# Local attention on Trainium2: the matmuls that spread the inverse sums become transposes and move ahead of the value products

## The chip, the cores and the metric

The kernel runs on one core of one Trainium2 chip. The metric is the device time of one execution in microseconds (us). Before the change it is 3235.11 us, the median of 3 runs (3233.68 to 3237.66). TensorE is PE here (its weight loads are PEld), VectorE is DVE, ScalarE is ACT, GpSimd is POOL, and SP issues most DMAs.

## What is computed

The whole program is two gated blocks of cross attention and feed-forward over 2048 tokens of 256 numbers. Only the last part is touched: a local transformer of two layers, each with windowed attention and a feed-forward. Cut to what matters, the reference is:

```python
def local_attention(q, k, v):                 # q, k, v: 8 heads, 2048 tokens, 64 numbers
    bq = q.reshape(b, h, w, WINDOW, d) * QK_SCALE      # WINDOW = 128, so 16 windows
    bk, bv = look_around(bk), look_around(bv)          # the window before and this one
    sim = jnp.einsum('bhwid,bhwjd->bhwij', bq, bk)
    sim = jnp.where(mask, -jnp.finfo(sim.dtype).max, sim)
    attn = jax.nn.softmax(sim, axis=-1)
    out = jnp.einsum('bhwij,bhwjd->bhwid', attn, bv)

# in a layer:
q, k = l2norm(q) * qs, l2norm(k) * ksc
q, k = rotary_xpos(q, k)
o = local_attention(q, k, v)
x = x + o.transpose(0, 2, 1, 3).reshape(b, n, INNER) @ wo
```

## The kernel before, in words

`windowed_attention` (L1885) runs once for each of the two layers and goes over 16 windows of 128 tokens. Each engine has its own instruction list, written out by hand as a loop over `w`; semaphores (`after`, L1911) tie the lists together, and nothing but the order of calls in each list sets the order of work on that engine. The loop is a software pipeline: in turn `w` TensorE computes the scores of window `w`, projects q, k and v of window `w + 3`, mixes the output of window `w - 1` with `wo`, turns the rotated q and k of window `w + 1`, turns the input of window `w + 4`, and then ends window `w`: `turn_probs` (L1994), `apply` (L2006), `spread` (L2021). All of it but the projections is float32; the projections are split into float16 halves. From `w = 12` on there is no input to turn, from `w = 13` on nothing is projected, and from `w = 14` on DVE has no q and k to prepare.

The softmax is not divided before the values are applied. `exp` (ACT, `expo`, L2065) leaves the sum of each row and head in `sums`; DVE takes their reciprocals (`invert`, L2187); POOL copies each of them 64 times along the free axis (`expand`, L2325); and `spread` on TensorE brings this `expanded` tile into the layout of the output, which has the heads' numbers on the partitions and the tokens along the free axis. It writes PSUM bank 7, `OUT_BANK`, which the turned input also uses. ACT copies the bank to SBUF (`move_spread`, L2075), and DVE multiplies `apply`'s result in PSUM by it (`normalize`, L2193). `mix` needs that product, and DVE's masks of the next window's scores (`mask`, L2201) stand behind it in DVE's list.

`spread` waits for POOL (`expanded`) and for ACT's copies of the turned input (`in_moved`). `apply` waits for ACT's copy of V (`valued`) and for the two halves of the turned probabilities (`probs_moved`). `score` of the next window comes after `spread` in TensorE's list and waits for `moved` and `probs_moved`; after half of its products it signals `scored`, for which the first mask waits.

```python
# ACT, turn w:  move_spread(w - 1); expo(w, 0); expo(w, 1); move(w + 1); move_input(w + 4);
#               square(w + 3); move_probs(w, 0); value(w + 3); move_probs(w, 1); root(w + 3)
# DVE, turn w:  make_unit(w + 2); normalize(w - 1); mask, maxima (w, 0); mask, maxima (w, 1);
#               add(w - 1); straighten(w + 2); rotate(w + 2); invert(w); sum_squares(w + 3)
```

Of the kernel before, what the change touches and what calls it, by code (L numbers as in the profile page):

```python
# [22 lines left out]
P = 128  # L23
# [1814 lines left out]
SCORE_BANK, QK_BANK, V_BANK, OUT_BANK = 3, 0, 2, 7  # L1838
# [46 lines left out]
def windowed_attention(nc, m, name, Z, pw, wm, w, l, s):  # L1885

    base = l * ST
    with ExitStack() as own:
# [16 lines left out]
        expanded = sb("expanded", [P, 4, 2, LD])  # L1905
# [5 lines left out]
        def after(engine, sem, count):  # L1911
            if count > 0:
                engine.wait_ge(s[sem], count)

        with nc.Block() as block:
# [5 lines left out]
            def _(pe):  # L1921
                def score(w):

                    after(pe, "moved", base + w + 1)
                    after(pe, "probs_moved", 2 * (base + w))
                    if w == 0:
                        after(pe, "united", base + 2)
                    last_slot, slot = (w - 1) % K_RING, w % K_RING
                    for c in range(4):
                        for e in range(2):  # L1930
                            rows = slice(64 * e, 64 * e + 64)
                            bank, at = SCORE_BANK + c // 2 * 2 + e, c % 2 * 2 * P
                            if last_slot < slot:
                                last = nc.tensor.matmul(m.PS[:, bank, at:at + 2 * P], qT[rows, c, :],
                                                        kT[rows, c, last_slot:slot + 1, :].rearrange("p o n -> p (o n)"),
                                                        start=True, stop=True)
                            else:
                                for j, sl in enumerate((last_slot, slot)):
                                    last = nc.tensor.matmul(m.PS[:, bank, at + j * P:at + (j + 1) * P], qT[rows, c, :],
                                                            kT[rows, c, sl, :], start=True, stop=True)  # L1940
                        if c % 2:
                            last.then_inc(s["scored"], 1)
# [10 lines left out]
                def project_qk(w):  # L1953

                    after(pe, "in_split", base + w + 1)

                    after(pe, "united", base + (w - 1 if w in (1, 2) else w))
                    for c in range(2):
                        last = project(m.PS[:, qk_bank(w) + c, :], w, c)
                    last.then_inc(s["qk_projected"], 1)  # L1960

                def project_v(w):

                    after(pe, "valued", base + w)
                    after(pe, "added", base + w - 3)
                    last = project(m.PS[:, V_BANK, :], w, 2)
                    last.then_inc(s["v_projected"], 1)

                def turn(w):

                    after(pe, "rotated", base + w + 1)
                    after(pe, "masked", 2 * (base + w) - 1)
                    for c in range(8):
                        last = nc.tensor.transpose(m.PS[:, SCORE_BANK + c // 4, (c % 4) * P:(c % 4 + 1) * P],
                                                   rotated[w % 2][:, c * P:(c + 1) * P], m.ident[:])
                    last.then_inc(s["turned"], 1)

                def turn_input(w):

                    after(pe, "normed", base + w - 4)  # L1980
                    after(pe, "in_moved", base + w)
                    for k in range(DK):
                        last = nc.tensor.transpose(m.PS[:, OUT_BANK, k * P:(k + 1) * P], Z[:, w, k * P:(k + 1) * P], m.ident[:])
                    last.then_inc(s["in_turned"], 1)

                def mix(w):

                    after(pe, "normed", base + w + 1)
                    for c in range(4):
                        last = nc.tensor.matmul(m.PS[:, V_BANK, 0:D], heads_outT[:, c, :], wo[:, c, :],  # L1990
                                                start=(c == 0), stop=(c == 3))
                    last.then_inc(s["mixed"], 1)

                def turn_probs(w, g):  # L1994

                    after(pe, "exped", 2 * (base + w) + g + 1)
                    if g == 0:
                        after(pe, "moved", base + min(w + 2, ST))
                    for p in range(4):
                        for kt in range(2):  # L2000
                            at = (p % 2 * 2 + kt) * P
                            last = nc.tensor.transpose(m.PS[:, SCORE_BANK + 2 * g + p // 2, at:at + P],  # L2002
                                                       probs[:, 4 * g + p, kt * P:(kt + 1) * P], m.ident[:])
                    last.then_inc(s["probs_turned"], 1)

                def apply(w):  # L2006


                    after(pe, "valued", base + min(w + 4, ST))
                    after(pe, "added", base + w)  # L2010
                    for c in range(4):
                        if c % 2 == 0:
                            after(pe, "probs_moved", 2 * (base + w) + c // 2 + 1)
                        for kt in range(2):
                            for e in range(2):
                                last = nc.tensor.matmul(m.PS[64 * e:64 * e + 64, V_BANK, c * P:(c + 1) * P],
                                                        V[:, (w - 1 + kt) % V_RING, 2 * c + e, :],
                                                        probsT[c // 2][:, c % 2 + 2 * e, kt, :], start=(kt == 0), stop=(kt == 1))
                    last.then_inc(s["applied"], 1)

                def spread(w):  # L2021

                    after(pe, "expanded", base + w + 1)
                    after(pe, "in_moved", base + min(w + 5, ST))
                    for c in range(4):
                        last = nc.tensor.matmul(m.PS[:, OUT_BANK, c * P:(c + 1) * P],
                                                expanded[:, c].rearrange("p e d -> p (e d)"), m.ident[:], start=True, stop=True)
                    last.then_inc(s["spread"], 1)

                turn_input(0)  # L2030
# [11 lines left out]
                for w in range(ST + 1):  # L2042
                    if inside(w):
                        score(w)
                    if inside(w + 3):
                        project_qk(w + 3)
                    if inside(w - 1):
                        if w == 1:
                            pe.wait_ge(s["rest_in"], 32 * (l + 1))
                        mix(w - 1)  # L2050
                    if inside(w + 1):
                        turn(w + 1)
                    if inside(w + 3):
                        project_v(w + 3)
                    if inside(w + 4):
                        turn_input(w + 4)
                    if inside(w):
                        for g in range(2):
                            turn_probs(w, g)
                        apply(w)  # L2060
                        spread(w)

            @block.scalar
            def _(act):
# [712 lines left out]
```

## Time and profile before

| | us |
|---|---|
| median of 3 runs | 3235.11 |
| the profiled execution's own time | 3229.91 |
| its span, from the first to the last instruction | 3227.8 |
| PE busy in the span | 2967.1 (92%) |
| DVE busy | 2208.0 (68%) |
| ACT busy | 1982.0 (61%) |
| POOL busy | 218.4 (7%) |
| mean granted TensorE clock | 0.975 of full speed |

The granted clock is a share of 2.4 GHz; a stretch at 1.2 GHz counts half. The first attention, which the change does not touch, takes some two thirds of the span. Windowed attention of the first layer lies at about 2435 to 2702 us, that of the second at about 2835 to 3098 us. A float32 matmul shows in the trace as two records for each one in the program, a transpose as one. A number in square brackets at the end of a row is the idle time of the engine just before it, with what ended it.

### The profile page before, as it was taken

How to read it: one execution, taken by the hardware profiler on the slowest of the kernel's cores; microseconds unless marked ns; L12 is line 12 of the kernel's file. 1: busy time of each engine (PE TensorE's matmuls, PEld its weight loads, DVE VectorE, ACT ScalarE, POOL GpSimd, SP SyncE). 2: the span in 40 equal slices, each digit the busy share in tenths (PEclk: the TensorE clock that was granted, in tenths of full speed). 3: DMA queues.
4: the chain of work that ended last, by engine and by line, in shares of the span. 5: the costliest groups of instructions: out<-in, count | busy, mean ns of one | idle time of the engine just before them, and what ended most of it. 6: DMA issues, size and time to landing. Idle time of an engine off the chain costs nothing. (4 is left out here: it accounts for less than half of the span.)

```text
span 3227.8 us, 71016 instructions
## 1 busy us (share of the span) xinstructions
PE 2967.1 (92%) x29442; PEld 1483.9 (46%) x29442; DVE 2208.0 (68%) x2752; ACT 1982.0 (61%) x2682; POOL 218.4 (7%) x325
## 2 busy tenths in 40 slices
PE   6999999999999999999999887999977887988878
PEld 3444444444444444444444563222235665556655
DVE  6888788878888888878788854000027775677756
ACT  5665655655656656556556424999965773267732
POOL 0000000000000000000000102000004223042200
PEclk8999999999999999999999898999998998999989
DMA  2000000000000000000000003110010001000000
GB/s 78 7 2 2 8 2 8 2 2 8 2 2 8 2 2 8 2 3 2 2 3 2 31 3 126 27 36 27 28 44 20 17 1 58 3 16 17 1 1 27
DMA packets 30033, 51.65 MB, mean 16 GB/s; under 512 B 6071, under 2 KB 22538, under 8 KB 28554
## 3 DMA queue, kind: packets, MB, share of 16 engines
q1 hardware_dynamic: 29706, 46.91, 4.6%
q8 instruction: 252, 4.13, 0.5%
q14 instruction: 75, 0.61, 0.1%
HBM read 41.04 MB, written 5.83 MB: 15 GB/s over the span
## 5 line engine op out<-in xcount | busy, mean ns | idle before, releaser
L734 ACT ACTIVATE a_probs<-PS 128x1024 f32<-128x1024 f32 x928 | 949.1, 1024 | 601.2 <-PE PS L489 597.4
L502 PE MATMUL PS<-a_probs,a_V 64*64 64x512 f32 x7424 | 977.8, 590 | 5.0 <-DVE a_heads_outT L915 3.6
L956 DVE TENSOR_TENSOR a_prob_sums<-a_prob_sums,a_probs 128x1024 f32<-128x1024 f32 x512 | 627.1, 1225 | 153.8 <-ACT a_probs L734 137.8
L953 DVE SCALAR_TENSOR_TENSOR a_prob_sums<-a_probs,a_valid,a_prob_sums 128x1024 f32<-128x1024 f32 x384 | 480.4, 1251 | 70.2 <-ACT a_probs L734 60.3
L489 PE MATMUL PS<-a_Q_hi,a_K_hi 64*64 64x512 f16 x3712 | 383.9, 381 | 5.0 <-ACT a_probs L734 4.7
L1772 ACT ACTIVATE c_probs<-PS 128x1024 f32<-128x1024 f32 (+1 forms) x416 | 382.8, 1080 | 8.3 <-PE PS L1691 6.7
L489 PE MATMUL PS<-a_Q_lo,a_K_hi 64*64 64x512 f16 x3712 | 383.5, 377 | 2.5 <-issue 2.5
L489 PE MATMUL PS<-a_Q_hi,a_K_lo 64*64 64x512 f16 x3712 | 381.1, 377 | 1.3 <-issue 1.3
L502 PEld LDWEIGHTS PS<-a_probs,a_V 64*64 64x64 f32 x7424 | 288.5, 133 | 164.1 <-issue 20.4
L489 PEld LDWEIGHTS PS<-a_Q_hi,a_K_hi 64*64 64x64 f16 x3712 | 118.4, 106 | 275.8 <-issue 270.7
L489 PEld LDWEIGHTS PS<-a_Q_hi,a_K_lo 64*64 64x64 f16 x3712 | 119.0, 107 | 228.3 <-issue 226.4
L1711 PE MATMUL PS<-c_probs,c_Vh 128*32 128x512 f32 (+1 forms) x1664 | 222.5, 607 | 0.3 <-ACT c_probs L1772 0.3
L1790 DVE COPY c_outT<-PS 128x512 f32<-128x512 f32 x16 | 11.1, 691 | 303.3 <-PE PS L1711 303.3
L1691 PE MATMUL PS<-c_Qop,c_Kop 64*128 64x512 f16 (+1 forms) x832 | 155.6, 390 | 34.6 <-ACT c_probs L1772 11.3
L2071 ACT ACTIVATE d_probs<-d_scores,d_minus_max 128x256 f32<-128x256 f32 x256 | 127.0, 497 | 88.2 <-DVE d_minus_max L2214 88.2
L489 PEld LDWEIGHTS PS<-a_Q_lo,a_K_hi 64*64 64x64 f16 x3712 | 120.0, 107 | 92.7 <-issue 7.8
L1691 PEld LDWEIGHTS PS<-c_Qop,c_Kop 64*128 64x128 f16 (+1 forms) x832 | 38.7, 94 | 250.9 <-ACT c_probs L1772 236.8
L923 DVE RECIPROCAL a_inverse<-PS 128x128 f32<-128x128 f32 x128 | 121.5, 950 | 27.1 <-PE PS L512 27.1
L71 POOL TENSOR_TENSOR b_W_lo<-b_W1T,b_W_hi 128x256 f16<-128x256 f32 x8 | 8.1, 1044 | 1830.9 <-DVE b_W_hi L67 1830.9
L2002 PE MATMUL PS<-ident,d_probs 128*128 128x128 f32 x512 | 70.3, 296 | 48.2 <-ACT d_kT L2086 41.5
L2310 POOL TENSOR_TENSOR d_crossed<-d_unit,d_tables 128x256 f32<-128x256 f32 x128 | 92.7, 758 | 147.8 <-DVE d_unit L2182 147.8
L2002 PEld LDWEIGHTS PS<-ident,d_probs 128*128 128x128 f32 x512 | 62.2, 153 | 56.2 <-issue 48.3
(325 smaller groups left out, 4227.5 us busy)
## 6 DMA issues: line engine op xcount, KB each, us to landing
c_Qop<-q_part SPq DMA_DIRECT2D x96, 64.0 KB, 2.3
c_Kop<-k_part SPq DMA_DIRECT2D x96, 50.0 KB, 2.0
d_raw<-in_l1f_w_dram SPq DMA_DIRECT2D x18, 256.0 KB, 3.2
d_tables<-in_rotary_dram SPq DMA_DIRECT2D x2, 2048.0 KB, 11.0
X<-in_x_dram SPq DMA_DIRECT2D x2, 1024.0 KB, 9.5
out_dram<-X SPq DMA_DIRECT2D x4, 512.0 KB, 3.5
c_cT<-in_ctxT_dram SPq DMA_DIRECT2D x1, 1601.0 KB, 6.4
a_probs<-in_ctx_dram SPq DMA_DIRECT2D x3, 512.0 KB, 5.0
```

The source lines that it names most:

```text
L489: last = nc.tensor.matmul(m.PS[64 * g:64 * g + 64, 2 * (n % 2) + h, :], k[rows, half_keys], q[rows, queries], start=(j == 0), stop=(j == l ...
L502: last = nc.tensor.matmul(m.PS[64 * h:64 * h + 64, PVB + g, :], V[e][rows, s, 64 * h:64 * h + 64], probs[n % 4][rows, h * BANK:(h + 1) * B ...
L734: nc.scalar.activation(probs[n % 4][:], m.PS[:, b0:b0 + 2, :].rearrange("p b c -> p (b c)"), ACT.Exp).then_inc(exped, 1)
L923: nc.vector.reciprocal(inverse[:, part], m.PS[:, TOTAL, part]).then_inc(inverted, 1)
L953: nc.vector.scalar_tensor_tensor(out=sums, in0=new, scalar=valid[:, s:s + 1], in1=sums, op0=ALU.mult, op1=ALU.add).then_inc(summed, 1)
L956: nc.vector.tensor_tensor(sums, sums, new, ALU.add).then_inc(summed, 1)
L1691: last = nc.tensor.matmul(m.PS[0:r, STEP_BANKS[n] + b, :], Kop[e][rows, c0:c0 + r], Qop[e][rows, q0:q0 + BANK], start=True, stop=True)
L1711: last = nc.tensor.matmul(m.PS[32 * q:32 * q + 32, 4 + e, :], Vh[e][0:r, t % CT, :], probs[2 * (t % 2) + q // 2][0:r, (q % 2) * BANK:(q % ...
L1772: nc.scalar.activation(probs[2 * (t % 2) + hp][0:r, :], m.PS[0:r, STEP_BANKS[n]:STEP_BANKS[n] + 2, :].rearrange("p b c -> p (b c)"), ACT.E ...
L2002: last = nc.tensor.transpose(m.PS[:, SCORE_BANK + 2 * g + p // 2, at:at + P], probs[:, 4 * g + p, kt * P:(kt + 1) * P], m.ident[:])
L2071: last = nc.scalar.activation(probs[:, p, :], scores[:, p, :], ACT.Exp, bias=minus_max[:, p:p + 1], accum_out=sums[:, p:p + 1])
L2310: last = nc.gpsimd.tensor_tensor(crossed[:, qk, :, a, :], unit[w % 2][:, qk, :, 1 - a, :], tables[:, 1, w, qk, a * 32:a * 32 + 32].unsquee ...
```

## The change

`spread` issues four transposes in place of four float32 matmuls with the same operands: `expanded` is the stationary operand and the identity the moving one, as before. And in TensorE's list `spread(w)` stands ahead of `apply(w)`, right behind `turn_probs(w, 1)`. No wait is added or removed; the lists of the other engines are as they were.

```diff
@@ -2023,8 +2023,8 @@
                     after(pe, "expanded", base + w + 1)
                     after(pe, "in_moved", base + min(w + 5, ST))
                     for c in range(4):
-                        last = nc.tensor.matmul(m.PS[:, OUT_BANK, c * P:(c + 1) * P],
-                                                expanded[:, c].rearrange("p e d -> p (e d)"), m.ident[:], start=True, stop=True)
+                        last = nc.tensor.transpose(m.PS[:, OUT_BANK, c * P:(c + 1) * P],
+                                                   expanded[:, c].rearrange("p e d -> p (e d)"), m.ident[:])
                     last.then_inc(s["spread"], 1)
@@ -2057,8 +2057,8 @@
                     if inside(w):
                         for g in range(2):
                             turn_probs(w, g)
+                        spread(w)
                         apply(w)
-                        spread(w)
```

TensorE's list at the end of an early window, with the turned input ahead and the next window's scores and projection behind (`d_probs` are the probabilities, `d_expanded` the copied inverse sums, `d_probsT` with `d_V` the value products, `d_kT` with `d_qT` the scores; x4 and the like count the program's operations):

```order
 L1983 MATMUL PS<-ident,d_Z 128x128 x2
 L2002 MATMUL PS<-ident,d_probs 128x128 x16
+L2026 MATMUL PS<-ident,d_expanded 128x128 x4
 L2016 MATMUL PS<-d_probsT,d_V 64x128 x16
-L2026 MATMUL PS<-ident,d_expanded 128x128 x4
 L1934 MATMUL PS<-d_kT,d_qT 128x256 x8
 L77 MATMUL PS<-qkv_hi,d_zw_lo 128x512
```

The four operations go from behind the value products to before them, so that the next window's scores follow the value products directly.

TensorE's list where a layer's projections have ended, from the close of window 12 to the close of window 13 (`d_wo` is the output matrix, `d_rotated` the rotated q and k):

```order
 L2002 MATMUL PS<-ident,d_probs 128x128 x16
+L2026 MATMUL PS<-ident,d_expanded 128x128 x4
 L2016 MATMUL PS<-d_probsT,d_V 64x128 x16
-L2026 MATMUL PS<-ident,d_expanded 128x128 x4
 L1934 MATMUL PS<-d_kT,d_qT 128x256 x8
 L1990 MATMUL PS<-d_wo,d_heads_outT 128x256 x4
 L1974 MATMUL PS<-ident,d_rotated 128x128 x8
 L2002 MATMUL PS<-ident,d_probs 128x128 x16
+L2026 MATMUL PS<-ident,d_expanded 128x128 x4
 L2016 MATMUL PS<-d_probsT,d_V 64x128 x16
-L2026 MATMUL PS<-ident,d_expanded 128x128 x4
```

The move is the same here, but no projections stand between the scores and the mix.

## Rows read from the trace of the kernel before

**Rows 1.** Windows: us, busy us per engine (PE, PEld, DVE, ACT, POOL), clock, DMA.
```profile
2542.29:2557.69 15.40, 13.78 (x110) 10.25 (x110) 12.13 (x17) 12.16 (x28) 4.54 (x8) 1.00 0.06 18
2650.06:2667.00 16.94, 12.04 (x90) 10.49 (x91) 9.17 (x11) 9.04 (x23) 3.52 (x6) 0.80 0.00 1
```

**Rows 2.** Timeline of ACT in one early window: start, duration, what [idle before].
```profile
2548.71 0.51 ACT L2071 ACTIVATE d_probs<-d_scores,d_minus_max 128x256 f32<-128x256 f32 x1 [0.31 <-DVE d_minus_max L2214]
...
2551.96 1.03 ACT L2104 ACTIVATE d_squares<-PS 128x1024 f32<-128x1024 f32 x1
...
2553.91 0.59 ACT L2111 ACTIVATE d_V<-PS 128x512 f32<-128x512 f32 x1
2554.39 1.03 ACT L2117 ACTIVATE d_probsT<-PS 128x1024 f32<-128x1024 f32 x1
...
2556.73 0.21 ACT L2124 ACTIVATE d_norms<-d_norms 128x16 f32<-128x16 f32 x1
2557.69 0.60 ACT L2079 ACTIVATE d_spread_in<-PS 128x512 f32<-128x512 f32 x1 [0.75 <-PE PS L2026]
```

**Rows 3.** Timeline of DVE, the window before and the start of the next.
```profile
2542.08 1.23 DVE L2182 TENSOR_TENSOR d_unit<-PS,d_norms 128x1024 f32<-128x1024 f32 x1
2543.22 0.68 DVE L2198 TENSOR_TENSOR d_heads_outT<-PS,d_spread_in 128x512 f32<-128x512 f32 x1
...
2556.98 0.17 DVE L2177 TENSOR_SCALAR d_norms<-d_norms 128x16 f32<-128x16 f32 x1 [1.68 <-ACT d_norms L2124]
```

**Rows 4.** Timeline of PE, and POOL's copy, in the same window as rows 2.
```profile
2551.70 0.74 POOL L2331 COPY d_expanded<-d_inverse 128x256 f32<-128x256 f32 x2 [5.54 <-DVE d_inverse L2191]
2551.89 1.94 PE L2002 MATMUL PS<-ident,d_probs 128*128 128x128 f32 x16 [0.90 <-ACT d_kT L2086]
2554.56 2.01 PE L2016 MATMUL PS<-d_probsT,d_V 128*64 128x128 f32 x32 [0.73 <-ACT d_V L2111]
2556.50 1.16 PE L2026 MATMUL PS<-ident,d_expanded 128*128 128x128 f32 x8
2557.59 2.00 PE L1934 MATMUL PS<-d_kT,d_qT 64*128 64x256 f32 x16
```

**Rows 5.** Who waited for L2026; what L2198 waited for (us, times).
```profile
  ACT d_spread_in L2079: 34.8, 32
...
  ACT d_spread_in L2079: 45.3, 6
```

**Rows 6.** Timeline, end of window 13 of the first layer.
```profile
2663.23 2.64 PE L2016 MATMUL PS<-d_probsT,d_V 128*64 128x128 f32 x32
2665.80 1.16 PE L2026 MATMUL PS<-ident,d_expanded 128*128 128x128 f32 x8
2666.89 2.00 PE L1934 MATMUL PS<-d_kT,d_qT 64*128 64x256 f32 x16
2667.00 0.60 ACT L2079 ACTIVATE d_spread_in<-PS 128x512 f32<-128x512 f32 x1 [2.64 <-PE PS L2026]
2667.63 0.69 DVE L2198 TENSOR_TENSOR d_heads_outT<-PS,d_spread_in 128x512 f32<-128x512 f32 x1 [8.29 <-ACT d_spread_in L2079]
2668.24 1.21 DVE L2206 TENSOR_TENSOR d_scores<-PS,d_masks 128x1024 f32<-128x1024 f32 x1
```

**Rows 7.** Timeline, window 15 of the first layer.
```profile
2692.10 1.97 PE L2002 MATMUL PS<-ident,d_probs 128*128 128x128 f32 x8 [1.29 <-ACT d_probs L2071]
...
2696.55 1.16 PE L2026 MATMUL PS<-ident,d_expanded 128*128 128x128 f32 x8
...
2698.37 0.69 DVE L2198 TENSOR_TENSOR d_heads_outT<-PS,d_spread_in 128x512 f32<-128x512 f32 x1 [6.09 <-ACT d_spread_in L2079]
```

**Rows 8.** Timeline of PE: the first 8 of a window's 16 score records.
```profile
2465.20 1.13 PE L1934 MATMUL PS<-d_kT,d_qT 64*128 64x256 f32 x8
```

**Rows 9.** Timeline of PE, end of window 13 of the second layer.
```profile
3057.26 3.56 PE L2002 MATMUL PS<-ident,d_probs 128*128 128x128 f32 x16 [4.90 <-ACT d_kT L2086]
3060.75 2.28 PE L2016 MATMUL PS<-d_probsT,d_V 128*64 128x128 f32 x32
```

## The prediction

> **What bounds the kernel now.** Only windowed attention changes, 16 windows in each of two layers, so I ask window by window which engine sets the pace. I read the busy time of single windows first, then the timelines of ACT, DVE and TensorE in one of them, then who waited for `spread`, and last the windows at a layer's end.
>
> An early window takes 15.40 us, and TensorE is busy for 13.78 us of it at the full clock [rows 1]. It looks like the bound and is not. ACT begins the second half of the exponentials when DVE has the second maxima (idle 0.31 us before), and from there its own list runs without a gap through the copies of q and k, the squares at 2551.96, V at 2553.91, the probabilities at 2554.39 and the square root at 2556.73, 0.21 us long [rows 2]. At 2556.98 DVE starts on the norms, having idled 1.68 us for that root [rows 3], and its list leads without a gap to the next maxima. So the loop is ACT, root, DVE, maxima, ACT. TensorE is in it nowhere: the one wait on `spread` is ACT's 0.75 us [rows 2], and it lies off the loop, because `normalize` cannot run before `make_unit` has ended. In the window of rows 3 the unit starts at 2542.08, and `normalize` follows at 2543.22 with no idle time. One window later the same place is 15.40 us on, at 2558.62, while ACT's copy is ready at 2557.69 + 0.60 = 2558.29 [rows 2]. The slack is 0.33 us already; more slack buys nothing.
>
> ACT waited for `spread` 32 times, 34.8 us in all, but DVE waited for ACT's copy only 6 times, 45.3 us in all [rows 5]. The 26 windows 0 to 12 of the two layers show the first wait alone; the six are windows 13, 14 and 15 of each layer. There no `make_unit` or other work of DVE covers it, and `normalize` ends an idle time of 8.29 us [rows 6]. Here `spread` is on the path: value products, `spread` from 2665.80, ACT's copy at 2667.00, `normalize` at 2667.63, first mask at 2668.24 [rows 6].
>
> **The change, part by part.** *Transposes for matmuls.* Four float32 matmuls are 8 records in 1.16 us [rows 4]; 16 transposes are 16 records in 1.94 us, and so four of them cost 1.94 / 4 = 0.49 us at the full clock. After idle time 8 transposes take 1.97 us [rows 7] and 16 take 3.56 us [rows 9], so four cost about 0.9 us at the half clock.
>
> *The move, windows 0 to 12.* `turn_probs` ends at 2553.83 and the value products wait for V until 2554.56, 0.73 us idle [rows 4]. The four transposes, 0.49 us, fit in. Their inputs are there: POOL's copy ends at 2551.70 + 0.74 = 2552.44 [rows 4], the input's copy precedes the squares of 2551.96. Value products end as before, and the scores start where `spread` did, at 2556.50 instead of 2557.59, 1.09 us earlier. What follows cannot use it: the next projection waits for `make_unit`, the mix for `normalize`, both of the loop. ACT copies the spread tile 0.75 us earlier and then waits 0.75 us longer for maxima. I count 26 windows at nothing. The cover is DVE's unit; were it gone, each window would gain at most ACT's 0.75 us, and I use that only for a rival. TensorE's new idle time comes in short pieces.
>
> *The move, windows 13 and 14, four times.* Nothing waits for V there. Call the present start of `spread` X (2665.80). The first mask starts at X + 2.44. Afterwards the four transposes come first and push the value products back. After 4.90 us of idle time TensorE is at 1.2 GHz there [rows 9], and the value products of 2.64 us, against 2.01 us in an early window, begin at the low clock and end at the high one [rows 4, 6]. The transposes take 0.9 us of the slow stretch, and the products they displace run later at twice the speed, so that the products end about 0.45 us later. The bounds are 0 (the second half of the products waits for ACT's copy anyway) and 0.9 us (nothing won back). The scores then start at X + 0.45. Two paths lead to the first mask: `normalize`, at once since ACT's copy of the spread is long done, over about X + 1.1; and half the scores, 1.13 us [rows 8] plus some 0.04 us for the signal, X + 1.62. The scores are late next. Gain 2.44 - 1.62 = 0.82 us, four times 3.3 us, and DVE, ACT and the next `turn_probs` pass it on since each waits for the one before.
>
> *Window 15, twice.* No scores follow. `normalize` now starts 2698.37 - 2696.55 = 1.82 us after X [rows 7]. Afterwards it waits for the products alone, which end some 0.07 us after X as the records overlap; with 0.45 us of delay and 0.04 us for the signal this is X + 0.56. Gain 1.26 us, twice 2.5 us. The mix, the last sum and the feed-forward wait for it and pass it on.
>
> **The sum** is 3.3 + 2.5 = 5.8 us. Against the profiled execution, 3229.91 us, this gives 3224.1 us. That execution lies 5.2 us below the median of the runs shown, so the same gain puts the median at 3229.3 us. With the bounds of the delay the gain is 3.0 us (0.9: four times 0.37 and twice 0.81) to 8.5 us (0: four times 1.27 and twice 1.71).
>
> **The clock, and a page that speaks against the change.** In window 13 of the second layer the 16 transposes take 3.56 us, nearly twice 1.94, and the value products right behind them 2.28 us, near to 2.01 [rows 4, 9]: TensorE came out of idle at 1.2 GHz, executed transposes alone, and went on at 2.4 GHz. Transposes thus bring the clock back. The Trainium skill, "TensorE: Matmul & The Clock Gate", Part 4: PE-mode transpose, says otherwise: the full clock does not engage for transposes, which do not count as activity in the way of matmuls. By that rule this change would take counted work away in each window; by the rows it takes none away. I follow the rows and keep the rule's outcome as a rival.
>
> **The rivals.**
>
> *Slower: the clock falls in the early windows.* `turn_probs`, `spread` and the idle time around them become one stretch with no matmul but transposes. If that lets the clock go to 1.2 GHz, the first 8 transposes of `turn_probs` end about 0.9 us later, and since ACT takes up the first half right behind the squares, at 2552.99, against their end near 2552.9, nearly all of it enters the loop. A window at a clock of 0.80 takes 16.94 us against 15.40 although it has less to do [rows 1]. At 0.9 to 1.5 us for 26 windows it costs 23 to 40 us: about 3235.1 + 31 - 5.8 = 3260 us. It decides from the point where the transposes of `turn_probs` take over 2.0 us. For it: the clock does fall where idle time grows to 4.90 us. Against: in an early window the idle time hardly grows (0.90 and 0.73 us now; the second is filled and similar pieces open elsewhere), and rows 9. Chance 0.05.
>
> *Faster by far: ACT is the bound after all.* If ACT's wait were on the loop, 26 windows would give 0.75 us each, 19.5 us, and the time would be 3210 us. For it: 34.8 us of waits on `spread`, the only wait of ACT on a product of this step. Against: ACT waits for DVE's maxima afterwards, and `normalize` shows no idle time in those windows [rows 3]. Chance 0.05.
>
> *No change: the ends give nothing.* The clock's falls and rises in windows 13 to 15 sit elsewhere in every pass. Window 13 costs 16.94 us [rows 1] against 15.40, so one badly placed slow stretch eats up to 1.5 us, and a few of them the gain. Or a transpose of `expanded` takes two passes as the matmul does; then the delay is at its upper bound and the gain 3 us. Against the latter: one record for each transpose in `turn_probs` [rows 4]. About 3234 us, chance 0.10.
>
> **How the numbers follow.** About 0.2%, 6.5 us, is what a measurement of this kernel can tell from no change. The forecast has 0.80. Its 5.8 us lies just inside that bound, its upper bound of 8.5 us outside, and three runs spread over 4 us; so I split it 0.33 faster, 0.45 same, 0.02 slower. The no-change case adds 0.09 same and 0.01 slower, the two large rivals 0.05 faster and 0.05 slower. Together: faster 0.38, same 0.54, slower 0.08. The range takes the gain from 8.5 us to about 1, with 2 us of scatter on the fast side: 3224.5 to 3234.5 us. Both large rivals are left out.
>
> **What would show it right or wrong.** Right: `spread` as 4 records ahead of the value products; early windows of 15.40 us at clock 1.00; ACT's wait on `spread` gone there and its wait for maxima longer by as much; `normalize` in windows 13 to 15 ended by the value products, with 0.8 us less to the mask in four of them and 1.3 us less in two. Wrong: early windows other than 15.40 us, `turn_probs` over 2 us in them, or a first mask that still waits for ACT's copy.

## The result and the profile after

The changed kernel takes 3229.62 us (median of 12 runs, 3224.11 to 3234.46) against 3235.59 us for the kernel before in the same session (12 runs, 3232.81 to 3239.30). The ratio is 0.9981 with an interval of 0.9972 to 0.9990: 6.0 us faster, just under the 0.2% that I named as the limit of what can be told from no change. The interval leaves out 1, so with twelve runs of each that limit was too wide. The forecast was 3229.3 us. In four of the twelve runs the changed kernel took 3234.2 to 3234.5 us at a mean granted clock of 0.970 to 0.971, against 0.973 to 0.976 in the others, and no trace shows where such a run loses the time.

| | before | after |
|---|---|---|
| profiled execution, us | 3229.91 | 3224.11 |
| span | 3227.8 | 3222.0 |
| PE records | 29442 | 29314 |
| mean granted clock | 0.975 | 0.974 |

128 records fewer are the 4 x 16 x 2 `spread` operations with one record each instead of two. The two spans differ by 5.8 us, the very sum of the prediction; the next views show that this agreement is partly luck.

An early window of the changed kernel, in the windows view (columns as in [rows 1]), and who waited for whom from 2465 to 2655 us, windows 1 to 12 of the first layer (us in total, times, longest), first in the kernel before and then in the changed one:

```profile
2542.94:2558.34 15.40, 13.34 (x106) 9.70 (x104) 12.07 (x16) 12.05 (x29) 4.52 (x8) 1.00 0.06 18
```
```profile
ACT d_probs L2071 <- DVE d_minus_max L2214: 31.4, 25, 2.1
...
ACT d_spread_in L2079 <- PE PS L2026: 9.7, 13, 0.7
```
```profile
ACT d_probs L2071 <- DVE d_minus_max L2214: 39.5, 24, 3.0
...
PE PS L77 <- DVE d_Z L2231: 4.2, 12, 0.3
PE PS L77 <- DVE d_unit L2182: 3.8, 12, 0.4
PE PS L2016 <- ACT d_V L2111: 3.5, 12, 0.3
```

The window is still 15.40 us at the full clock. TensorE's wait for V fell from 0.73 us [rows 4] to 0.29, and the time comes back as short waits of the projections (L77) for `make_unit` and for `add`. ACT's wait on `spread`, 9.7 us before, is gone, and its waits for maxima have gone from 31.4 us to 39.5 us instead. The same place in the timeline of the changed kernel:

```profile
2553.73 1.94 PE L2002 MATMUL PS<-ident,d_probs 128*128 128x128 f32 x16 [1.07 <-ACT d_kT L2086]
...
2555.51 0.60 PE L2026 MATMUL PS<-ident,d_expanded 128*128 128x128 f32 x4
...
2556.40 2.01 PE L2016 MATMUL PS<-d_probsT,d_V 128*64 128x128 f32 x32 [0.29 <-ACT d_V L2111]
...
2558.34 2.00 PE L1934 MATMUL PS<-d_kT,d_qT 64*128 64x256 f32 x16
2558.58 0.22 ACT L2124 ACTIVATE d_norms<-d_norms 128x16 f32<-128x16 f32 x1
2558.70 0.58 ACT L2079 ACTIVATE d_spread_in<-PS 128x512 f32<-128x512 f32 x1
```

ACT's copy now follows the root at once. Windows 13 and 14 of the first layer:

```profile
2661.52 3.64 PE L2002 MATMUL PS<-ident,d_probs 128*128 128x128 f32 x16 [5.06 <-ACT d_kT L2086]
...
2664.96 0.95 PE L2026 MATMUL PS<-ident,d_expanded 128*128 128x128 f32 x4
...
2665.85 1.97 PE L2016 MATMUL PS<-d_probsT,d_V 128*64 128x128 f32 x32
2666.12 0.59 ACT L2079 ACTIVATE d_spread_in<-PS 128x512 f32<-128x512 f32 x1
2667.75 2.00 PE L1934 MATMUL PS<-d_kT,d_qT 64*128 64x256 f32 x16
2667.92 0.69 DVE L2198 TENSOR_TENSOR d_heads_outT<-PS,d_spread_in 128x512 f32<-128x512 f32 x1 [6.70 <-issue]
2668.93 1.23 DVE L2206 TENSOR_TENSOR d_scores<-PS,d_masks 128x1024 f32<-128x1024 f32 x1 [0.32 <-PE PS L1934]
...
2684.13 0.69 DVE L2198 TENSOR_TENSOR d_heads_outT<-PS,d_spread_in 128x512 f32<-128x512 f32 x1 [8.00 <-PE PS L2016]
```

The copy of the spread tile ends at 2666.71, more than 1 us before `normalize`, which waits for the value products; and the first mask has a new wait, 0.32 us, for half the scores. That is the new path of the prediction, and its mask comes 2668.93 - 2667.75 = 1.18 us after the scores start, against 1.17 predicted.

One label has to be read with care. Of what `normalize` (L2198) waited for in the changed kernel (us, times) the trace says:

```profile
  PE PS L2016: 22.8, 4
  issue: 6.7, 1
  ACT d_spread_in L2079: 6.3, 1
```

The last row is window 13 of the second layer. There the copy had ended at 3059.99 and `normalize` began at 3060.88, so the value products were what it waited for. One wait of six for two semaphores is put down to the wrong one.

Where the 5.8 us of the span are I read from the starts of `normalize`. In the kernel before that of window 12 starts at 2650.99 us in the first layer, that of window 15 at 2698.37; in the changed kernel at 2652.86 and 2695.87:

| stretch, us | before | after |
|---|---|---|
| to `normalize` of window 12, first layer | 2650.99 | 2652.86 |
| from there to window 15, first layer | 47.38 | 43.01 |
| on to window 12 of the second layer | 350.23 | 350.35 |
| from there to window 15, second layer | 45.84 | 42.40 |
| on to the end | 133.4 | 133.4 |

The two tails gave 7.8 us, not 5.8, and the part ahead, whose code is the same, took 1.9 us more in this pass. I judge the change by the tails below, since a whole run scatters by several microseconds ahead of them.

### The profile page after: what moved, and what is told of

Read it like the earlier page. It is cut to its first block and busy times, and to the rows that moved or that the text cites. A ratio compares the mean times of both kernels' runs of the same rounds, so it can differ in the third digit from the quotient of the medians.

```text
span 3222.0 us, 70760 instructions
## 1 busy us (share of the span) xinstructions
PE 2949.9 (92%) x29314; PEld 1465.9 (45%) x29314; DVE 2207.8 (69%) x2752; ACT 1978.7 (61%) x2682; POOL 218.6 (7%) x325
## 5 line engine op out<-in xcount | busy, mean ns | idle before, releaser
L489 PEld LDWEIGHTS PS<-a_Q_lo,a_K_hi 64*64 64x64 f16 x3712 | 120.4, 107 | 90.8 <-issue 6.0
L77 PE MATMUL PS<-qkv_hi,d_zw_lo 128*128 128x512 f16 x192 | 75.2, 392 | 28.4 <-DVE d_unit L2182 16.7
```

What stands on the lines that cost most here:

```text
L77: nc.tensor.matmul(out, sl, mh, start=start, stop=False)
L489: last = nc.tensor.matmul(m.PS[64 * g:64 * g + 64, 2 * (n % 2) + h, :], k[rows, half_keys], q[rows, queries], start=(j == 0), stop=(j == l ...
```

## The experiments

Tail is the sum of both layers' stretches from `normalize` of window 12 to that of window 15, in the profiled execution. Each kernel was timed with the kernel before on the same chip; medians of three sessions of before are 3234.93, 3234.03 and 3235.91 us. The ratios are not the quotients of the medians and differ from those by up to 0.0006.

| run | median us (runs) | ratio to before, interval | tail, us |
|---|---|---|---|
| before, first trace | | | 93.2 |
| r_before_again | 3234.69 (11) | 0.9998, 0.9989 to 1.0007 | 92.7 |
| changed, first trace | 3229.62 (12) | 0.9981, 0.9972 to 0.9990 | 85.4 |
| r_after_again | 3227.11 (11) | 0.9979, 0.9970 to 0.9988 | 85.9 |
| r_move_only | 3233.43 (11) | 0.9996, 0.9987 to 1.0005 | 92.3 |
| r_transpose_only | 3230.78 (11) | 0.9991, 0.9982 to 1.0000 | 90.6 |
| r_ends_only | 3227.94 (11) | 0.9987, 0.9978 to 0.9996 | 85.8 |
| r_early_only | 3229.66 (11) | 0.9987, 0.9978 to 0.9996 | 90.8 |
| r_double_early | 3252.03 (5) | 1.0057, 1.0043 to 1.0071 | 95.9 |
| r_double_late | 3232.45 (11) | 0.9988, 0.9979 to 0.9997 | 85.5 |
| r_fill_transposes | 3222.97 (5) | 0.9965, 0.9951 to 0.9978 | 81.9 |
| r_fill_matmuls | 3224.75 (6) | 0.9966, 0.9954 to 0.9978 | 80.4 |
| r_fill_all | 3219.42 (5) | 0.9949, 0.9935 to 0.9962 | 76.5 |
| r_fill_all_old_order | 3227.00 (8) | 0.9975, 0.9964 to 0.9985 | 84.0 |

### Both kernels a second time

> The changed kernel as it is, a second time, for the share of chance in its trace. In the first trace the three last windows of a layer, from normalize of window 12 to normalize of window 15, went from 47.4 to 43.0 us in the first layer and from 45.8 to 42.4 us in the second, 7.8 us in all against 5.8 predicted, and the code ahead of the local attention, the same in both kernels, took 1.9 us more. Theory A (the price of the step is 5.8 us, the rest is where the clock's falls happen to lie): the sum of the two tails differs from the first trace by up to 2 us, the early windows are again 15.40 us, the median is 5 to 7 us under before. Theory B (the tails gain 7.8 us by the order alone): both tails come out within 0.3 us of the first trace. Theory C, ACT's wait counted: the early windows would be under 15.40 us.

> The kernel before, profiled a second time, since its three last windows were seen only once (47.4 and 45.8 us from normalize of window 12 to that of window 15). Theory A (part of the 7.8 us was where the clock fell in that pass): the sum of the two tails differs from 93.2 us by 1 us or more, and the second half of turn_probs in window 15, which ran at the low clock in both layers, is at the full clock in one of them. Theory B: both tails within 0.3 us of the first trace.

The tails nearly repeat: 43.4 and 42.5 us changed, 46.8 and 45.8 us before. On the second traces of each the gain is 6.8 us, on the first 7.8. Neither theory is met to the letter. B asked for 0.3 us, and two of the four tails lie 0.4 and 0.5 us from their first trace; A asked of the kernel before for a sum 1 us away and for a second half at the full clock, and the sum is 0.5 us away, with both halves as they were. In size the gain is that of B, and "by the order alone" is not shown: part of it is the clock. Window 15 shows why 5.8 us was too little. Its two halves of `turn_probs`, before (first fence, the second trace of the kernel before) and changed (second trace of the changed kernel):

```profile
2689.86 1.09 PE L2002 MATMUL PS<-ident,d_probs 128*128 128x128 f32 x8 [2.06 <-ACT d_probs L2071]
2692.25 1.97 PE L2002 MATMUL PS<-ident,d_probs 128*128 128x128 f32 x8 [1.29 <-ACT d_probs L2071]
2694.14 2.54 PE L2016 MATMUL PS<-d_probsT,d_V 128*64 128x128 f32 x32
```
```profile
2697.37 1.09 PE L2002 MATMUL PS<-ident,d_probs 128*128 128x128 f32 x8 [1.90 <-ACT d_probs L2071]
2699.75 1.09 PE L2002 MATMUL PS<-ident,d_probs 128*128 128x128 f32 x8 [1.29 <-ACT d_probs L2071]
2700.79 0.66 PE L2026 MATMUL PS<-ident,d_expanded 128*128 128x128 f32 x4
2701.38 1.97 PE L2016 MATMUL PS<-d_probsT,d_V 128*64 128x128 f32 x32
```

Before, the second half ran at 1.2 GHz in both layers of both traces. In the changed kernel it ran at 2.4 GHz in both layers of both traces, and so it did in r_ends_only and r_double_late: 8 windows out of 8 with transposes ahead of the products there, none out of 4 before. (Windows 13 and 14 of these kernels have no extra work; with it the clock fell in window 15 too, see below.) With the matmuls ahead of the products, r_move_only, the clock fell within the second half in both layers, after the same idle times of 1.90 and 1.29 us. With transposes behind the products (r_transpose_only and r_early_only) it was at 2.4 GHz in two of four windows, and in the other two the clock fell within it.

### One part of the change at a time

```diff
 # r_move_only, against the kernel before
+                        spread(w)        # still matmuls
                         apply(w)
-                        spread(w)
 # r_transpose_only: the other half of the change, matmul -> transpose, order as before
```

> The old matmuls, moved ahead of the value products. Theory A: at the low clock eight records in place of four cost about 1.8 us instead of 0.9 before the value products; half of what is displaced is won back at the high clock, so the products end 0.9 us late instead of 0.45. Gain four times 0.37 and twice 0.81 us, 3.1 us, early windows 15.40 us still, since eight records at 1.16 us end 0.4 us after V is there and the 1.0 us of room ahead of the scores covers that. Theory C (ACT's wait is on the loop): early windows 14.7 us, gain about 19 us. If the number of passes does not matter the gain is that of the full change, 5.8 us.

> Transposes in place of the matmuls, still behind the value products. The chain of windows 13 to 15, products, spread, ACT's copy, normalize, is kept and only its spread is shorter, 0.5 to 0.6 us instead of 1.16. Theory A: 0.5 to 0.6 us in each of six windows, 3 to 3.6 us in all, early windows 15.40 us with ACT's wait down from 0.74 to about 0.2 us. Theory C: 26 times 0.55 us more, 17 to 18 us in all. If transposes let the clock fall, early windows above 15.40 us.

The early windows are 15.40 us in both, which is against theory C. The move alone takes 0.6 us off the tail, less than the 3.1 us forecast, and its time cannot be told from no change. Against the mean of the two traces of before, windows 13 and 14 lose 0.5 us over the four, from the start of `turn_probs` to the first mask, where 1.5 us were forecast as a gain, and window 15 gains 1.2 us of the 1.6. In its window 13 the eight cold records take the 1.8 us expected:

```profile
2665.27 3.65 PE L2002 MATMUL PS<-ident,d_probs 128*128 128x128 f32 x16 [5.06 <-ACT d_kT L2086]
2668.71 1.81 PE L2026 MATMUL PS<-ident,d_expanded 128*128 128x128 f32 x8
2670.45 1.97 PE L2016 MATMUL PS<-d_probsT,d_V 128*64 128x128 f32 x32
2672.35 2.00 PE L1934 MATMUL PS<-d_kT,d_qT 64*128 64x256 f32 x16
```

From `turn_probs` to the scores that is 7.08 us, against 6.23 with transposes (2661.52 to 2667.75). The transposes alone take 2.4 us off the tail (forecast 3 to 3.6) and 4.2 us off the median. Of the 2.4 us, 2.0 lie in window 15, and 1.6 of those in the second layer, where its second half ran at the full clock. So the two parts alone give 3.0 us, the two together 7.3 us, but the clock's falls are in each of these figures, from one trace each, and how the gain divides between transposes and order is not shown.

### Where the gain lies

```diff
 # r_ends_only, against the changed kernel; r_early_only has the two conditions exchanged
-                        spread(w)
+                        if w >= 13:
+                            spread(w)
                         apply(w)
+                        if w < 13:
+                            spread(w)
```

> Transposes, moved ahead of the value products in windows 13 to 15 only; windows 0 to 12 keep them behind. Theory A: all that the order is worth lies in the last three windows, so this gives what the full change gives, 6 to 8 us under before, with early windows of 15.40 us. Theory D (the earlier scores and projections of windows 0 to 12 are worth something too, through the state in which they hand over to window 13): 1 us or more is missing against the full change.

> Transposes, moved ahead of the value products in windows 0 to 12 only; the last three windows have them behind. Theory A: the move is worth nothing there, so this equals transposes without a move, about 4 us under before by the last measurement and 3 by the working. Theory D: more than that, 5 us and up.

With the move in windows 13 to 15 alone the tail is 85.8 us, that of the full change; with the move in windows 0 to 12 alone it is 90.8 us, that of r_transpose_only. The medians go the same way, 6.1 and 4.4 us under before, but the intervals of the two ratios are the same; the tails, 5.0 us apart, separate what the timing cannot. Nothing is missing against the full change, so theory D falls. Of the 5.0 us, part is again the clock in window 15.

### How much slack the early windows have

```diff
 # r_double_early on the kernel before, r_double_late on the changed one (with its transpose)
-                    for c in range(4):
+                    for c in range(8 if w < 13 else 4):
+                        c %= 4
```

> The kernel before, with the four matmuls of spread issued twice in windows 0 to 12, so 1.09 us more on TensorE there; the result is the same. This measures the slack by which I called the early windows free. Theory A: 0.33 us of slack in normalize, the rest of 1.09 us enters the loop, 0.76 us for 26 windows, 20 us slower, normalize now idle until ACT's copy. Theory C (no slack): 1.09 us for 26 windows, 28 us slower. If TensorE is nowhere near the loop, no change.

> The changed kernel with its four transposes issued twice in windows 0 to 12. The counterpart of the doubled matmuls behind the products, which cost 17 us. Theory A: 0.44 us more ahead of the products, of which 0.29 us go into TensorE's wait for V; the products end 0.15 to 0.2 us late, and 1.5 us of slack to the mask hide that: no change to the changed kernel, early windows 15.40 us. If the place ahead of the products is on the loop, up to 0.44 us for 26 windows, 11 us slower.

Doubling behind the products costs 17.1 us, doubling ahead of them nothing that the trace shows: early windows stay at 15.40 us and the tail is 85.5 us. The timing shows that less well: the median is 3.5 us under before, where the changed kernel lay 6.0 and 7.8 us under it in other sessions, and the runs scatter over 11 us. In r_double_early a window takes 16.00 us, 0.61 us more, in this way:

```profile
2545.64 2.05 PE L2027 MATMUL PS<-ident,d_expanded 128*128 128x128 f32 x16
...
2546.62 1.22 DVE L2183 TENSOR_TENSOR d_unit<-PS,d_norms 128x1024 f32<-128x1024 f32 x1
...
2547.73 0.60 ACT L2080 ACTIVATE d_spread_in<-PS 128x512 f32<-128x512 f32 x1 [1.64 <-PE PS L2027]
...
2548.36 0.69 DVE L2199 TENSOR_TENSOR d_heads_outT<-PS,d_spread_in 128x512 f32<-128x512 f32 x1 [0.51 <-ACT d_spread_in L2080]
```

Sixteen records take 2.05 us against 1.16 for eight, so the addition is 0.89 us and not the 1.09 us I used (which holds the change-over to the scores as well). 0.89 - 0.61 = 0.28 us was slack, against the 0.33 read from the rows. That is the place where ACT's wait on `spread` starts to count, and the change moved away from it.

The 26 windows at 0.61 us come to 15.8 us. The tail of r_double_early, 95.9 us, is another 2.9 us longer than the mean of the two of before, though nothing in windows 13 to 15 was edited. The clock sat elsewhere in it: the value products took 3.68 us in window 15 of the first layer, against 2.62 and 2.54 us before, and 3.05 us in windows 13 and 14 of the second, against 2.28 and 2.6. So a tail repeats for one kernel, but an edit ahead of it can move it by 3 us through the clock alone, and differences of tails of that size (r_move_only, r_transpose_only) are not the price of a step by themselves.

### What holds the clock

```diff
+                def fill():
+                    for i in range(32):
+                        c = i % 4
+                        nc.tensor.transpose(m.PS[:, QK_BANK, c * P:(c + 1) * P], m.ident[:], m.ident[:])
...
+                    if w in (13, 14):
+                        fill()        # r_fill_matmuls: 16 float32 matmuls of the identity
                     if inside(w):
                         for g in range(2):
                             turn_probs(w, g)
```

> The changed kernel, and in windows 13 and 14 TensorE turns the identity 32 times into a PSUM bank that is free there, in its idle time of 5.06 and 4.46 us ahead of turn_probs; the result is the same. At the full clock that is 32 times 0.11, 3.5 us. If transposes keep the clock up, as the rows of window 13 of the second layer say, the 16 transposes of turn_probs take 1.94 us instead of 3.65 and spread 0.6 instead of 1.0: 1.5 to 2 us for each of four windows, 6 to 8 us under the changed kernel, some 3221 us. If transposes do not count as activity the clock falls as before, the 32 take up to 7 us at the low clock, and turn_probs begins late: 2 to 3 us for each of four windows slower, some 3238 us.

> As the run with 32 transposes, but with 16 float32 matmuls of the identity in their place, 32 records and the same 3.5 us at the full clock. Both views expect the clock to stay up here: 6 to 8 us under the changed kernel. If only matmuls count, this run alone gains; if both count, the two are within 1 us of each other.

Window 13 with the extra transposes (L2034), and then window 15 of the same kernel:

```profile
2657.83 3.66 PE L2034 MATMUL PS<-ident 128*128 128x128 f32 x32
2663.05 1.94 PE L2002 MATMUL PS<-ident,d_probs 128*128 128x128 f32 x16 [1.57 <-ACT d_kT L2094]
2664.83 0.60 PE L2026 MATMUL PS<-ident,d_expanded 128*128 128x128 f32 x4
2665.36 1.97 PE L2016 MATMUL PS<-d_probsT,d_V 128*64 128x128 f32 x32
...
2688.93 1.97 PE L2002 MATMUL PS<-ident,d_probs 128*128 128x128 f32 x8 [1.29 <-ACT d_probs L2079]
2690.69 1.06 PE L2026 MATMUL PS<-ident,d_expanded 128*128 128x128 f32 x4
2691.68 3.56 PE L2016 MATMUL PS<-d_probsT,d_V 128*64 128x128 f32 x32
```

With nothing but transposes in the gap, `turn_probs` takes 1.94 us and not 3.64, as it does with matmuls in it. Windows 13 and 14 take 13.04 and 13.47 us with either filling; the tails, 81.9 and 80.4 us, differ only in window 15 of the first layer. Transposes hold the clock. The Trainium skill, "TensorE: Matmul & The Clock Gate", Part 4: PE-mode transpose, states the contrary, that the full clock does not engage for transposes since they do not count as busy time in the same way. Its durations there are for bf16 and these transposes are float32; for these the measurement decides against it. Against the changed kernel windows 13 and 14 of both layers save 8.9 us together, but only 3.5 us of it remain in the tail, because window 15 now falls to the low clock, as in the kernel before. So the 6 to 8 us expected were not reached in the tail, and by the medians, 3222.97 us against the changed kernel's 3227.11 and 3229.62, the gain is 4.1 to 6.7 us. The two fillings were expected within 1 us of each other, and their medians are 1.8 us apart.

The last pair fills window 15 too, in the new order and in the old (`fill` now takes the number of transposes):

```diff
+                    if w >= 13 and inside(w):
+                        fill(32 if w < 15 else 12)
                     if inside(w):
                         for g in range(2):
+                            if w == 15 and g:
+                                fill(8)
                             turn_probs(w, g)
```

> The changed kernel with 32 extra transposes of the identity in windows 13 and 14, as in the run before, and also in window 15: 12 ahead of the first half of turn_probs and 8 ahead of its second half, in idle times of 1.90 and 1.29 us, whose clock fell in both traces with filled windows 13 and 14. If that fall came from those two idle times, window 15 takes 11.7 us from normalize to normalize in place of 14.45, so 2.7 us in each layer less than with windows 13 and 14 filled: some 3217.5 us. If the extra work at the end rather delays the exponentials' followers or the fall comes anyway, 3223 us or more.

> The kernel before (matmuls, behind the value products) with the same extra transposes. With the clock at full speed in all six windows of both kernels, the difference to the changed kernel with the same filling is the price of the order and the transposes alone. Theory A: at the full clock four transposes cost 0.5 us ahead of the products; the first mask comes at X + 0.5 + 1.18 in place of X + 2.44, four times 0.76 us, and the last normalize at X + 0.6 in place of X + 1.82, twice 1.2 us: 5.5 us between the two, and this one near 3223 us. Theory B (the 7.8 us of the first trace were the price of the order): 7.8 us between the two.

Window 15 goes to 11.74 us, and r_fill_all, at 3219.42 us, is the fastest kernel here: 16.5 us under before, and its tail is 16.4 us shorter than the mean of the two of before. Together the two runs take the clock out of the comparison: it is 1.00 from window 12 to window 15 in both layers of both. The difference of tails is 7.5 us, not the 5.5 I had expected, and that of the medians 7.6 us. This is the price of the whole change, transposes and order together; the pair does not divide it. Window 13 in the old order and in the new:

```profile
2663.64 1.94 PE L2002 MATMUL PS<-ident,d_probs 128*128 128x128 f32 x16 [1.42 <-ACT d_kT L2096]
...
2665.90 1.97 PE L2016 MATMUL PS<-d_probsT,d_V 128*64 128x128 f32 x32 [0.33 <-ACT d_probsT L2127]
2667.80 1.16 PE L2026 MATMUL PS<-ident,d_expanded 128*128 128x128 f32 x8
```
```profile
2666.07 1.94 PE L2002 MATMUL PS<-ident,d_probs 128*128 128x128 f32 x16 [1.57 <-ACT d_kT L2096]
...
2667.85 0.60 PE L2026 MATMUL PS<-ident,d_expanded 128*128 128x128 f32 x4
2668.38 1.97 PE L2016 MATMUL PS<-d_probsT,d_V 128*64 128x128 f32 x32
...
2670.27 2.00 PE L1934 MATMUL PS<-d_kT,d_qT 64*128 64x256 f32 x16
```

In the old order the products wait 0.33 us for ACT's copy of the first half; X is 4.16 us after the start of `turn_probs`. In the new one the transposes fill that wait, and the scores start after 4.20 us. At the full clock the delay is 0.04 us, my lower bound of 0, and not 0.5. The first mask comes 6.60 us after the start of `turn_probs` in the old order and 5.39 us in the new, 1.21 us for each of four windows. Window 15 gives the rest; old order first:

```profile
2689.54 1.09 PE L2002 MATMUL PS<-ident,d_probs 128*128 128x128 f32 x8 [0.75 <-ACT d_probs L2081]
...
2696.98 0.69 DVE L2208 TENSOR_TENSOR d_heads_outT<-PS,d_spread_in 128x512 f32<-128x512 f32 x1 [4.87 <-ACT d_spread_in L2089]
```
```profile
2689.57 1.09 PE L2002 MATMUL PS<-ident,d_probs 128*128 128x128 f32 x8 [0.59 <-ACT d_probs L2081]
...
2695.66 0.69 DVE L2208 TENSOR_TENSOR d_heads_outT<-PS,d_spread_in 128x512 f32<-128x512 f32 x1 [3.52 <-PE PS L2016]
```

From `turn_probs` to `normalize` that is 7.44 us against 6.09, 1.35 us for each of two windows. Four times 1.21 and twice 1.35 are the 7.5 us.

## Why the prediction was right, and where a term was off

The time lies in the range and near its middle, the early windows did nothing, and the ends gave the gain by the path foretold. That the figure came so near is in part luck, since two terms were off in opposite directions. By its steps:

**Windows 0 to 12 cost and gain nothing.** Right. They are 15.40 us in both kernels; r_early_only shows no gain of the move there and r_double_early puts the slack at 0.28 us. The faster rival, ACT's waits being on the loop, falls with them: in r_transpose_only and the changed kernel these waits shrink or go, and the windows stay at 15.40 us.

**Four transposes 0.49 us, at the low clock 0.9 us.** Right: from the start of `spread` to that of the products it is 0.53 us in window 13 at the full clock (2664.83 to 2665.36) and 0.89 us at the low one (2664.96 to 2665.85).

**Value products 0.45 us late.** Right as a mean only. From the start of `turn_probs` to X, then to the new start of the scores, the four windows give a delay of 0.08, 0.59, 0.12 and 1.35 us, 0.54 in the mean. The last has a longer `turn_probs` in it: 2.90 us before, 3.65 after, by where the clock fell, and nearly the same in the second traces (2.92 and 3.65). At the full clock the delay is 0.04 us.

**First mask 1.17 us after the scores, four times 0.82 us.** The path is right. From the start of `turn_probs` to the first mask the four windows gave 1.18, 0.66, 1.13 and -0.11 us, 2.9 us against 3.3, and in the second pair of traces 0.65, 0.33, 1.07 and -0.17 us, 1.9 us. At the full clock it is 1.21 us for each, 4.8 us, so here the clock took away a part of what the change gives.

**Window 15, twice 1.26 us.** This is the term that was mis-sized. From the start of `turn_probs` to `normalize` it took 8.65 and 8.54 us before and 6.09 us in both layers after: 5.0 us in place of 2.5. About half of it is the change at an equal clock, 1.35 us for each layer, near to the 1.26 forecast, as the pair at the full clock shows. The other half, 2.3 us, is the clock, which no longer falls between the two halves of `turn_probs`. I had put the clock's falls down to chance, good for a loss as for a gain; in window 15 the full clock goes with the change, 8 windows of 8 where windows 13 and 14 have no extra work. With the idle times there filled (r_fill_all and r_fill_all_old_order) it did not fall in 4 windows of 4, in either order. Why 2.06 and 1.29 us of idle time let it fall in the kernel before while 1.90 and 1.29 us do not in the changed one is open: in r_move_only, and with windows 13 and 14 filled, it fell at 1.90 and 1.29 us as well, so the length of the gaps is not the whole reason.

**The sum.** 5.8 us predicted; the tails gave 7.8 and 6.8 us in two pairs of traces, the medians 6.0 and 7.8 us in two sessions. Windows 13 and 14 gave less than forecast (2.9 and 1.9 us for 3.3), window 15 more (5.0 and 4.9 us for 2.5). The lower bound of the gain was added up as 3.0 us; its terms give 3.1. The equal figure of 5.8 us between the two first spans is 7.8 us of gain less 1.9 us of scatter ahead of the local attention, and is no proof of the sum.

**The slower rival**, the clock falling in early windows because of the transposes, did not occur, and r_fill_transposes takes its reason away. **The no-change rival** did not come about: the falls of the clock do not sit elsewhere in every pass, since the tails of each kernel repeat within 0.6 us. They do move when the windows ahead get longer, by 2.9 us in r_double_early.

## What to carry to other kernels

Total waiting time does not tell what a wait is worth: 32 waits on one step came to 34.8 us, and only the six whose release started the next engine had a price. Look for the windows where a pipeline runs empty, since cover that holds in 26 windows is missing there. Work that fits into a wait of its own engine should be put there, and a gap that lets TensorE's clock fall can be worth more than the step that follows it. To price an edit of such a place, compare the two orders with the clock held up in both, as the last pair does.

## What the runs showed of the hardware

Transposes hold TensorE at 2.4 GHz and bring it back, as float32 matmuls do: 16 transposes of 128 x 128 take 1.94 us after 32 others and 3.64 us after 5.06 us of idle time. In window 13 of the second layer of the changed kernel the clock comes back with transposes alone:

```profile
3054.89 3.55 PE L2002 MATMUL PS<-ident,d_probs 128*128 128x128 f32 x16 [5.06 <-ACT d_kT L2086]
3058.28 0.60 PE L2026 MATMUL PS<-ident,d_expanded 128*128 128x128 f32 x4
```

The granted clock is 0.51 in the first row and 1.00 in the second, and no matmul lies between. A float32 matmul of 128 x 128 by 128 columns takes two records, a transpose of the same shape one, and at the full clock each record takes some 0.11 us of TensorE's time (0.89 us for the eight added in r_double_early). Extra work of no use in TensorE's idle time, 168 transposes in all, made the kernel 7.7 to 10.2 us faster than the changed one by the medians of its two sessions (3227.11 and 3229.62 against 3219.42 us), and its tail 8.9 us shorter (85.4 against 76.5).
